# A two-layer graph network: row numbers copied once a round for two rounds, and ScalarE's single rows in layer 0

## What is computed

```python
# layer 0
t1 = feat @ W1
msg = t1[src] + feat[src] * feat[dst] @ W2
msg = msg / (jnp.sqrt(out_deg[src]) * jnp.sqrt(out_deg[dst]))[:, None]
embed = where(in_cnt > 0, t1 + segment_sum(msg, dst), 0) + b
embed = leaky_relu(embed, 0.01)
embed = embed / max(norm(embed), 1e-12)
x = layernorm(x + embed)
# layer 1
xt = x @ W.T + b
x = layernorm(x + segment_sum(xt[src], dst) / (deg + 1)[:, None])
```

## Time and profile before

| | us |
|---|---|
| median of 3 runs | 3900.78 (3900.3 to 3907.59) |
| profiled execution, its own time | 3905.06 |
| its span, first to last instruction | 3902.9 |
| PE busy | 2713.0 (70%) |
| VectorE (DVE) busy | 1913.0 (49%) |
| ACT busy | 547.6 (14%) |
| POOL busy | 2908.9 (75%) |

### The profile page before, as it was taken

The page is one execution under the profiler, slowest core; times in us unless marked ns, Lnnn a source line. Parts: engine busy times, 40 slices in busy tenths (PEclk is TensorE's granted clock), DMA queues, the critical chain, the costliest instruction groups (busy, mean ns, idle before and its releaser), DMA issues.

```text
span 3902.9 us, 63900 instructions
## 1 busy us (share of the span) xinstructions
PE 2713.0 (70%) x10186; PEld 1859.7 (48%) x10186; DVE 1913.0 (49%) x3812; ACT 547.6 (14%) x1836; POOL 2908.9 (75%) x3066
## 2 busy tenths in 40 slices
PE   4551777666767676666777777777777777777777
PEld 3440555555656565555534443434444434444443
DVE  8995466666666666666532323333333333333333
ACT  8992000000000000000100000000000000000000
POOL 7776777777777777777757777777777777777776
PEclk5555888888888888888867777777777777777777
DMA  7878455555555555555534444444444444444443
GB/s 252 271 240 319 142 164 164 162 164 163 164 162 163 161 164 160 163 159 164 151 88 121 125 125 126 123 128 123 126 122 128 122 127 121 128 123 126 122 128 106
DMA packets 322784, 594.31 MB, mean 152 GB/s; under 512 B 71073, under 2 KB 207062, under 8 KB 322582
## 3 DMA queue, kind: packets, MB, share of 16 engines
q0 software_dynamic: 146208, 399.44, 35.8%
q1 hardware_dynamic: 149938, 171.30, 13.2%
q10 hardware_dynamic: 26436, 21.80, 1.8%
HBM read 506.29 MB, written 75.48 MB: 149 GB/s over the span
## 4 chain that ended last, share of the span: by engine, by line
POOL 37%; issue 21%; SPq 20%; DMA 4%; ACTq 2%; PE 2%; DVE 2%; DVEq 1%; POOLq 0%; ACT 0%
POOL ring L580 37%; SPq L459 14%; SPq L452 4%; ACTq L762 2%; PE banks L1335 2%; DMA src_lo<-scaled_x 1%; DMA ring<-x,idx 1%; DVEq L866 1%; DMA x_t<-in_x 1%; DMA ring<-src_lo 1%; SPq L386 1%; SPq L432 1%; SPq L381 1%; PE banks L1303 0%; ACTq L742 0%
## 5 line engine op out<-in xcount | busy, mean ns | idle before, releaser
L1335 PE MATMUL banks<-ring,hot_space 128*128 128x257 f32 x6252 | 2098.5, 474 | 587.5 <-DMA ring<-x,idx 463.6
L1335 PEld LDWEIGHTS banks<-ring,hot_space 128*128 128x128 f32 x6252 | 1282.2, 227 | 1326.1 <-DMA ring<-x,idx 934.3
L580 POOL DMA_INDIRECT ring<-x,idx x1517 | 1440.3, 949 | 487.6 <-issue 458.8
L580 POOL DMA_INDIRECT ring<-scaled_x,idx x1247 | 1194.4, 958 | 399.7 <-issue 381.5
L1042 DVE SCALAR_TENSOR_TENSOR big<-banks,here_mask,big 128x257 f32 x784 | 343.0, 479 | 1417.3 <-PE banks L1335 1414.1
L988 DVE TENSOR_TENSOR hot_space<-banks,dst_rel 128x1024 f32<-128x1024 f32 x345 | 421.9, 1224 | 173.0 <-issue 171.3
L1292 PE MATMUL banks<-ident,halves 128*128 128x128 f32 x588 | 147.6, 413 | 416.4 <-DVE halves L1056 414.1
L702 ACT COPY idx<-src_col 128x8 int32 (+1 forms) x392 | 77.0, 197 | 2479.9 <-PE banks L1335 1525.0
L1292 PEld LDWEIGHTS banks<-ident,halves 128*128 128x128 f32 x588 | 112.3, 215 | 460.1 <-DVE halves L1056 409.7
L590 POOL DMA_INDIRECT ring<-in_x,src_col x276 | 264.0, 956 | 84.1 <-issue 84.1
L665 ACT ACTIVATE dst_rel<-columns,halves 128x128 bf16<-128x128 f32 x960 | 268.3, 372 | 5.5 <-DVE halves L901 5.5
(11 more groups left out here) (123 smaller groups left out, 1228.9 us busy)
## 6 DMA issues: line engine op xcount, KB each, us to landing
src_lo<-scaled_x SPq DMA_DIRECT2D x2944, 1.0 KB
src_lo<-x SPq DMA_DIRECT2D x2944, 1.0 KB
src_lo<-x ACTq DMA_DIRECT2D x2944, 1.0 KB
kept_rows<-ring SPq DMA_DIRECT2D x94, 384.0 KB, 3.3
ring<-kept_rows SPq DMA_DIRECT2D x47, 768.0 KB
ring<-x,idx POOLq DMA_INDIRECT x1517, 4.1
src_lo<-scaled_x ACTq DMA_DIRECT2D x1408, 1.0 KB
ring<-scaled_x,idx POOLq DMA_INDIRECT x1247, 2.8
```

Of the source, the lines that this page charges most:

```text
L580: g.indirect_dma_start(ring[:, u, 0:D], None, table[layer], bass.IndirectOffsetOnAxis(ap=idx[:, u:u + 1], axis=0)).then_inc(rows_in[u], 16)
L1335: last = nc.tensor.matmul(group_sum(k % SUMS), dst_hot[:, k % HOTS, u - k * GT, :], ring[:, u, 0:DW], start=u == tiles[0], stop=u == tiles ...
```

## The change

The row numbers of a round are copied at once, 32 columns, into one of two halves of `idx`, a round ahead (`next_idx`). POOL waits once a round for them and then waits for each group of the round before by itself. POOL's loop holds four rounds in both layers. In layer 0 ACT brings the last tile of each odd round from 3, with the same order and the same blocks of rows as in layer 1: 24, 8, 16 and 16 rows a round. In a round the row numbers are now read ahead of the pass of a whole tile. The diff, cut to its core:

```diff
-FEW = (ROUNDS - 1) // SPAN - 1
-ACT_BLOCKS = (((0, 16), None, None, (16, 32)), ((0, 24), (24, 32), (32, 48), (48, 64)))
+SPANS = (ROUNDS - 1) // SPAN - 1
+ACT_BLOCKS = ((0, 24), (24, 32), (32, 48), (48, 64))
-        idx = sb("idx", [P, U], I32)
+        idx = sb("idx", [P, 2, U], I32)
...
+            def gather_round(layer, i, n, end=U, first=0, ahead=True):
+
+                g.wait_ge(idx_ready, layer * ROUNDS + i + 1)
+                g.sem_inc(gather_turn, 1)
+                for q in range(4):
+                    if ahead:
+                        g.wait_ge(groups_done, group_no(layer, i - 1, q) + 1)
+                        g.sem_inc(gather_turn, 1)
+                    for u in range(max(q * QT, first), min((q + 1) * QT, end)):
+                        g.indirect_dma_start(ring[:, u, 0:D], None, table[layer],
+                                             bass.IndirectOffsetOnAxis(ap=idx[:, idx_buf(layer, n), u:u + 1],
+                                                                       axis=0)).then_inc(rows_in[u], 16)
...
+                    first = 0 if layer else KEPT
+                    gather_round(layer, 0, 0, ahead=layer == 1)
+                    gather_round(layer, 1, 1, first=first)
+                    for i in range(2, SPAN):
+                        gather_round(layer, i, i, HAND_U, first)
+                    with g.Fori(1, SPANS + 1) as h:
+                        for n in range(SPAN):
+                            gather_round(layer, SPAN * h + n, n, HAND_U, first)
+                    gather_round(layer, ROUNDS - 1, ROUNDS - 1, FINAL)
...
-            def refill(layer, i, q):
-
-                act.wait_ge(groups_done, group_no(layer, i, q) + 1)
-                act.sem_inc(act_turn, 1)
-                nc.scalar.copy(idx[:, q * QT:(q + 1) * QT],
-                               src_col[:, bass.ds(i * U + U + q * QT, QT)]).then_inc(idx_ready, 1)
+            def next_idx(layer, i, n):
+
+                if layer or not (isinstance(i, int) and i == 0):
+                    act.wait_ge(groups_done, group_no(layer, i - 1, GR - 1) + 1)
+                    act.sem_inc(act_turn, 1)
+                first = 0 if isinstance(i, int) and i == ROUNDS - 1 else i * U + U
+                nc.scalar.copy(idx[:, idx_buf(layer, n + 1), :],
+                               src_col[:, bass.ds(first, U)]).then_inc(idx_ready, 1)
...
+            def round_(layer, i, n, sums, ended, last=False, hand=None, half=0, passed=None):
+
+                first_row = half * 2 * HAND_ROWS
+                if hand is not None:
+                    if half == 0:
+                        hand_loaded(layer, hand)
+                    starts = load_starts(layer, hand, 2 * half, False)
                 if passed is not None:
                     pass_hand(layer, passed)
...
+                if hand is not None:
+                    if half == 0:
+                        hand_free(layer, hand)
+                    hand_block(layer, first_row, 0, starts)
+                if not (last and layer):
+                    next_idx(layer, i, n)
+                if ended:
+                    roots(layer, i - 2)
+                if hand is not None:
+                    hand_block(layer, first_row, 1, starts)
+                if sums and layer == 0 and not last:
+                    clear_sums(i - 1)
+                if sums and layer == 1:
+                    act.wait_ge(groups_added, group_no(layer, i, LAST_K + 1) + SUMS)
+                    take_sums(i - 1, acc[:, bass.ds(2 * i - 2, 2), :])
+                if hand is not None:
+                    starts = load_starts(layer, hand, 2 * half + 1,
+                                         half == 1 and not (isinstance(hand, int) and hand == HANDS))
+                    hand_block(layer, first_row, 2, starts)
+                if sums:
+                    take_turned(layer, i - 1)
+                if hand is not None:
+                    hand_block(layer, first_row, 3, starts)
...
+                    round_(layer, 0, 0, False, False)
+                    round_(layer, 1, 1, True, False, hand=1)
+                    with act.Fori(1, HANDS) as h:
+                        round_(layer, 2 * h, 0, True, True, hand=h, half=1)
+                        round_(layer, 2 * h + 1, 1, True, True, hand=h + 1, passed=h)
+                    round_(layer, 2 * HANDS, 0, True, True, hand=HANDS, half=1)
+                    round_(layer, 2 * HANDS + 1, 1, True, True, passed=HANDS)
+                    round_(layer, ROUNDS - 1, ROUNDS - 1, True, True, last=True)
...
                     if layer == 0:
-                        round_(layer, 2, True, with_kept=True, find=True, over=0, h=1)
-                        round_(layer, 3, True, with_kept=True, find=True, plain=3)
...
+                        with pe.Fori(1, HANDS) as h:
+                            for over in range(2):
+                                round_(layer, 2 * h + over, True, with_kept=True, find=True, over=over, h=h)
+                        round_(layer, 2 * HANDS, True, with_kept=True, find=True, over=0, h=HANDS)
+                        round_(layer, 2 * HANDS + 1, True, with_kept=True, over=1, h=HANDS)
```

## The result

| | before | after |
|---|---|---|
| median of the runs, us | 3904.19 (3900.3 to 3911.45) | 4273.32 (4268.31 to 4277.03) |
| profiled execution, us | 3905.06 | 4270.87 |
| its span, us | 3902.9 | 4268.7 |

The changed kernel takes 1.0944 times as long as the one before, interval 1.0931 to 1.0957. The forecast was 4234 us; the median lies 39 us above it and inside the range.

A forecast was written before the change was run, and what follows sets the result against it. It took SP's queue to bound layer 0 and POOL layer 1, with ACT's order bounding layer 0 afterwards. Rounds summed to 1793.7 us against 1462.0, 331.7 more; 3905.06 + 333 = 4238 profiled, 4234 us median, range 4130 to 4340.

The forecast's parts named there:

- Its distance between SP and POOL: Layer 0 before the change: SP needs 64.9 us for two rounds, POOL only 1.3 us less.
- Removed work at nothing: Twelve POOL gathers in layer 0 (15.1 us of POOL) and three of four index copies a round, gathers gaining nothing off-bound.
- Even rounds, 38.1 us: Layer 0 rounds where ACT's loop turns: 26.8 us from clearing copy to root, plus 11.3 to the next clearing copy.
- Odd rounds, 41.7 us: Layer 0 rounds where ACT passes a whole tile: 30.4 us from clearing copy to root, plus 11.3 to the next.
- the landing of rows ahead of the pass: ACT's wait in odd rounds of layer 0 for its rows to land, 4.7 us, with a reading of row numbers under it.
- The loop, not the work: ACT's program order before the root sets layer 0; rival: ACT's own work alone, 69.9 us per two rounds, 4014 us, chance 0.07.
- VectorE's cover: Layer 0: VectorE is ready for the root 24.8 us after the clearing copy at the latest, ACT at 26.8.
- the rival in which it falls: PE's clock drops from 0.82 to 0.5, VectorE is ready last in layer 0: 4483 us, chance 0.1 for a third or more.
- some 8: POOL in layer 0 would idle some 8 us a round, needing 31.5 us a round for 25 gathers.
- The turn of the loop: ACT's loop turning at each even round of layer 0 was kept at 2.7 us, possible values 0 to 3.
- SP as the bound after: Rival: ACT has slack and SP's 64.9 us for two rounds of layer 0 stand: 3901 us, no change, chance 0.03.
- the gain from 12 gathers: Rival: POOL bounds layer 0 after all, so the removed gathers save 15 us: 3886 us, chance 0.05.

The follow-up runs named there:

- Index copies alone: Changed kernel with ACT's and POOL's hands of layer 0 as in the kernel before, 32 rows a round: 3900.46 us, ratio 0.9996.
- the unrolled run: Kernel before with three hands in a turn of SP's loop and row numbers read ahead of the wait for a free hand: 3903.72 us, ratio 0.9989.
- the rows alone: Kernel before, with ACT gathering the last tile of every odd round of layer 0 and four index copies a round kept: 4306.67 us, ratio 1.1032.
- 24 rows fewer: Changed kernel with ACT leaving out all 24 rows of the first block in each round of layer 0: 3973.4 us, ratio 1.017.
- 8 rows fewer: Changed kernel with ACT leaving out 8 of the first block's 24 rows in each round of layer 0: 4127.56 us, ratio 1.0565.
- roots and copies ahead: Changed kernel, layer 0: index copy and roots ahead of the first 24 rows, turned-half copies ahead of the second reading and its rows: 3967.32 us, ratio 1.0162.
- the run with half the turns: Changed kernel with two hands in each turn of ACT's loop, so it turns in every second even round: 4234.42 us, ratio 1.0844.

## Why the prediction was right, and where it was off

**The bound before.** It put layer 0 on SP and layer 1 on POOL. Index copies alone changed nothing, which fits. Its distance between SP and POOL (1.3 us in 64.9) was a little too large. A gather is 1.26 us as foretold (1.264 from one to the next in the unrolled run, 800 to 1800 us), 63.8 us for 50.5. From round 3 to round 43 two rounds take 64.9 us before and 64.0 with SP's loop unrolled, so POOL is some 1.0 us behind. This didn't touch the sum, as neither was the bound after. The expectation for the unrolled SP was off by about 25 us all the same. Of the 16.1 us that its rounds gained, 8.4 came back at the end of the layer, where POOL had lost its lead; the expectation had no term for that. The profiled execution, the fastest of its 11, is 7.8 us under that of the kernel before, and the medians measured side by side differ by 4.6.

**Removed work at nothing.** The 12 gathers and three index copies a round were costed at 0 as long as SP or ACT bounds. Index copies alone: 0.9996. They were not quite 0 once ACT bounds: 33 us lie between the rows alone and the change, with the place of the reading in them. The sum had both in its terms (0.4 us a round off for copies, the reading under the landing).

**Even rounds, 38.1 us.** Measured 38.4 on the mean. 26.8 from t to root became 27.1, 11.3 from root to t became 11.32. All terms stand: 24 rows, a second reading, the turn.

**Odd rounds, 41.7 us.** Measured 43.2 as the mean of the 22 between round 1 and round 46 (43.4 in the middle of the layer). Here one term was mis-sized: the landing of rows ahead of the pass. The prediction took the landing of the kernel before over unchanged, 4.7 us (a mean of 4.5 over its 11 passes). In the changed kernel it is 1297.36 + 5.14 to 1308.57, 6.07 us, and 21 of 23 passes lie between 5.6 and 6.4. Over the 22 odd rounds it is 5.9 us on the mean, 1.5 more than before, and that is the whole 1.5 us by which those rounds are longer than foretold. In 22 rounds that is 32.6 us, and 0.27 us in 23 even rounds are 6.2: together the 38.8 us between 370.5 and 331.7.

Why a landing became longer is not settled. With the index copies alone, where ACT's rows are as before, it is 4.5 us on the mean. With the rows alone it is 5.2 (median), and in each kernel that has both 5.9 to 6.3. It is not the number of rows a round: with 24 rows fewer ACT issues 40 a round, not 64, and the landing is still 6.1 us. What the kernels with a long landing share, the rows alone among them, is 32 rows issued right ahead of the wait where the kernel before issues 16. That may account for 4.5 to 5.2. The kernels with both also read row numbers between the last row and the wait and copy the index once a round; the single copy by itself leaves the landing at 4.5. Which of these makes the rest no run separates. What was off is that a wait for DMAs was carried over although the change alters what is issued right ahead of it.

**The loop, not the work.** Root to t held at 11.32 us. Moving rows behind the root shortened the round by what they took. Taking rows off did so too in odd rounds, and in even ones by the turn on top, until SP's load of x (8 rows fewer), VectorE (24 rows fewer) or ACT's own work and SP's (roots and copies ahead) came next.

**VectorE's cover.** "Ready at 24.8 at the latest" is 22.2 us in the trace, and it waits 10.10 us in the odd round. The clock stayed at 0.79 of full in the stretch, against 0.82, and the rival in which it falls did not come up.

**SP and POOL.** SP has time over and loads x 3.0 to 3.3 us after the root, when the variance is there. POOL stands 7.12 and 12.05 us once a round; "some 8" was about right. In layer 1 it waits for nothing, with the same 0.3 us as in rows 12:

```profile
POOL ring L588 <- issue: 386.5, 1267, 0.3
```

**The turn of the loop.** The prediction kept 2.7 us, the runs show 2.8 to 3.0. The Trainium skill (Advanced Engine Details and Errata, Control Flow Timing) puts a branch that is always taken at some 0.05 us and a compare and branch, which is what ends this loop, at some 0.11. By that the forecast would have been 57 to 59 us lower, and the run with half the turns, 39 us faster for 11 turns fewer, speaks against it. The trace has 0.05 us for the branch itself and 2.79 us of nothing behind it. The run with 8 rows fewer shows that a turn can also be short, 0.2 us behind the branch.

**The rivals.** SP as the bound after and the gain from 12 gathers both needed ACT to hide its rows; it can't in any order tried. The Trainium skill (Perfetto Trace Analysis, DMA Optimizations) says that spreading DMAs over the engines that can issue them may help where the generation of their descriptors is the bound. Here ACT, the engine with the most room on the page, 14% busy before, took 32 rows more a round and the kernel lost 9%. The rows came from POOL, which was not the bound of layer 0, so this case does not refute that sentence. It shows what the sentence leaves out: the issues must not stand ahead of a step that others wait for.

## What to carry to other kernels

An engine that looks idle may stand in a loop that ties the rounds together: before giving it DMAs to issue, find the step of it that others wait for, and count every issue, reading and wait that program order puts ahead of that step, at their step and not at their busy time. Put such work behind that step, where the engine only waits, as eight rows behind the root cost nothing and eight ahead of it cost 2.5 us a round. When two engines pace a loop within 2% of each other, as SP and POOL do here, freeing one gives only the distance to the other, and a lead that the other had at the end of the loop is lost; measure that distance as a mean over many rounds. And price a wait for DMAs anew when the change alters what is issued right ahead of it.

## What the runs showed of the hardware

The turn of a long loop on ACT costs 2.8 to 3.0 us on its queue, in one program with and without it (14.80 and 17.83 us for the same 39 rows). Nearly all of it is a gap right behind the branch: 2.4 to 3.0 us in layer 0 of the change, 0.22 us in every turn with 16 rows fewer in the body. On ACT and SP this gap is over 2 us or under 0.5 in every turn of the traces. The length of the body alone does not decide. The traces have 304 instructions in the long one and 272 in the short one, but 306 in ACT's loop of layer 1, where the median gap is 2.71 us in the change and 0.19 with the index copies alone. On SP it is of the same kind. Two passes (line 469) and what follows them in the kernel before with SP's loop unrolled, first over a turn, then without one:

```profile
1240.86 0.55 SPq L469 DMA_DIRECT2D ring<-src_lo  x1
1245.46 0.61 SPq L432 DMA_DIRECT2D ring<-kept_rows  x1
...
1305.24 0.55 SPq L469 DMA_DIRECT2D ring<-src_lo  x1
1306.07 0.58 SPq L432 DMA_DIRECT2D ring<-kept_rows  x1
```

From the pass to the next issue it is 4.05 us with the turn and 0.28 without.

A single row of 1 KB costs its queue 0.33 to 0.34 us in the bursts of 15 to 24 rows shown for the change (the length of a burst over its rows). The wait for such rows to land was 4.5 us on the mean behind 16 rows in the kernel before and 5.9 behind 32 in the change.
